# GpSimd's queue in a feature-interaction kernel: the three sums of a block first, then the gathers and stores of another block

## The reference

```python
e = jnp.stack([tbl_0[ids[:, 0]], ..., tbl_39[ids[:, 39]]], axis=1)      # 512 x 40 x 32
h = e
for i, (W, bias) in enumerate(params):                                   # three layers of 200
    x = jnp.einsum('bhd,bmd->bhmd', h, e).reshape(B, -1, D)
    y = jax.nn.relu(jnp.einsum('oi,bid->bod', W, x) + bias[None, :, None])
    if i != n_layers - 1:
        h, direct = jnp.split(y, 2, axis=1)
    else:
        direct = y
    outs.append(direct)
z = jnp.concatenate(outs, axis=1).sum(-1)
h = jnp.maximum(jnp.concatenate([z, dense_ctx], axis=1) @ W_top1 + b_top1, 0.0)
y = jnp.maximum(h @ W_top2 + b_top2, 0.0) @ W_top3
```

## Time and profile before

| | us |
|---|---|
| median of three runs | 2821.92 (2819.53 to 2822.87) |
| the profiled execution, its own time | 2822.93 |
| its span in the trace | 2821.1 |
| PE busy | 2775.4 (98% of the span) |
| DVE busy | 2637.9 (94%) |
| ACT busy | 1500.6 (53%) |
| GpSimd busy | 858.7 (30%) |
| DMA issued by GpSimd (queue q0), share of 16 engines | 12.1% |

### The profile page before, as it was taken

One profiled execution on the slowest core, in us unless ns is written; L12 is line 12 of the kernel. 1 busy time (PEld: TensorE's weight loads), 2 busy tenths in 40 slices (PEclk: granted clock), 3 DMA queues, 4 the chain that ended last, 5 costly groups with the idle time before them and its releaser, 6 DMA issues.

```text
span 2821.1 us, 54038 instructions
## 1 busy us (share of the span) xinstructions
PE 2775.4 (98%) x19012; PEld 2758.2 (98%) x19012; DVE 2637.9 (94%) x1945; ACT 1500.6 (53%) x1880; POOL 858.7 (30%) x700
## 2 busy tenths in 40 slices
PE   5999999999999999999999999999999999999999
PEld 4999999999999999999999999999999999999997
DVE  6999999999999999999999999999999999999995
ACT  4555555555555555555555555555555555555553
POOL 5433332332332332332323323323323323333100
PEclk9999999999999999999999999999999999999999
DMA  7333333433433433333334334334333334334330
GB/s 210 85 83 84 86 94 78 94 87 76 99 88 75 100 84 82 97 84 85 93 79 94 87 78 97 89 75 102 85 78 99 85 82 95 85 86 94 85 78 18
DMA packets 286025, 249.66 MB, mean 89 GB/s; under 512 B 31286, under 2 KB 284446, under 8 KB 285893
## 3 DMA queue, kind: packets, MB, share of 16 engines
q1 hardware_dynamic: 216310, 200.56, 25.4%
q0 software_dynamic: 65712, 45.56, 12.1%
q10 hardware_dynamic: 3972, 3.17, 0.4%
HBM read 140.74 MB, written 4.20 MB: 51 GB/s over the span
## 4 chain that ended last, share of the span: by engine, by line
PE 94%; POOL 2%; DVE 1%; DMA 1%; issue 1%; SPq 0%; ACT 0%; another core or an unknown queue 0%; DVEq 0%; ACTq 0%; POOLq 0%
PE acc L809 62%; PE acc L811 29%; POOL gathered L445 1%; PE z_ps L826 1%; PE hid_ps L822 1%; DVE tails L721 1%; DMA acc_copy<-acc_copy 1%; DVE product L716 1%; PE acc L880 0%; SPq L380 0%; DMA gathered<-in_table,rows_all 0%; PE hid_ps L903 0%; DMA hid_rep<-hid 0%; ACT acc_copy L528 0%
## 5 line engine op out<-in xcount | busy, mean ns | idle before, releaser
L809 PE MATMUL acc<-weights,heads 126*128 126x400 f32 (+1 forms) x9088 | 2694.1, 364 | 16.3 <-DVE tails L721 16.2
L811 PE MATMUL acc<-weights,tails 126*128 126x200 f32 (+1 forms) x9088 | 2321.6, 255 | 0.0
L522 ACT ACTIVATE heads<-product 126x1024 fp32r<-126x1024 f32 (+2 forms) x1152 | 1198.1, 1047 | 1021.5 <-PE acc L811 507.3
L811 PEld LDWEIGHTS acc<-weights,tails 126*128 126x128 f32 (+1 forms) x9088 | 1740.8, 192 | 0.0
L809 PEld LDWEIGHTS acc<-weights,heads 126*128 126x128 f32 (+1 forms) x9088 | 1712.9, 188 | 19.7 <-issue 10.0
L721 DVE TENSOR_TENSOR tails<-product,heads 126x1024 fp32r<-126x1024 f32 (+2 forms) x1152 | 1348.9, 1204 | 1.4 <-ACT heads L522 1.1
L716 DVE TENSOR_TENSOR product<-hid_rep,x_rep 126x2048 f32<-126x2048 f32 x510 | 1167.4, 2289 | 96.5 <-PE acc L811 64.8
L453 POOL DMA_DIRECT2D acc_copy<-acc_copy x189 | 235.0, 1244 | 1719.8 <-ACT acc_copy L528 1716.4
L445 POOL DMA_INDIRECT gathered<-in_table,rows_all x320 | 510.8, 1596 | 101.4 <-issue 97.1
L536 ACT ACTIVATE y_relu<-acc_copy 128x400 f32<-128x400 f32 x192 | 102.4, 533 | 217.0 <-DMA acc_copy<-acc_copy 215.0
L528 ACT ACTIVATE acc_copy<-acc 128x800 f32<-128x800 f32 x192 | 158.7, 827 | 9.8 <-PE acc L811 7.7
(11 more groups left out here) (26 smaller groups left out, 118.2 us busy)
## 6 DMA issues: line engine op xcount, KB each, us to landing
x_rep<-x_rows SPq DMA_DIRECT2D x512, 120.0 KB
hid_rep<-hid SPq DMA_DIRECT2D x511, 120.0 KB
x_pairs<-x_rows SPq DMA_DIRECT2D x191, 280.0 KB
acc_copy<-acc_copy POOLq DMA_DIRECT2D x189, 200.0 KB
hid_rep<-hid SPq DMA_DIRECT2D x511, 5.0 KB
x_pairs<-x_rows SPq DMA_DIRECT2D x63, 120.0 KB
gathered<-in_table,rows_all POOLq DMA_INDIRECT x320
raw_weights<-in_w SPq DMA_DIRECT2D x8, 500.0 KB, 6.1
```

Of the source, the lines that this page charges most:

```text
L522: act.activation(heads[0:rows, ring % HEADS_RING, 0:tiles, :], product[0:rows, ring % PRODUCT_RING, 0:tiles, :], ACT.Copy).then_inc(heads_ ...
L809: nc.tensor.matmul(acc[:, at.parity, c, 0:2 * LAYER], dims(heads[0:rows, ring % HEADS_RING, k, :], c), w, start=(q == 0 and k == 0), stop= ...
L811: last = nc.tensor.matmul(acc[:, at.parity, c, LAYER:2 * LAYER], dims(tails[0:rows, ring % PRODUCT_RING, k, :], c), w[:, 0:LAYER], start=F ...
```

## The change

GpSimd issues all three sums of a block before its gathers and stores. Before, the first sum stood ahead of the gathers, and the second and third between the gathers and the stores; for block 5 alone one gather stood ahead of the first sum. No instruction is added or removed, and the other engines' lists stay as they are.

```diff
             for b in range(FIRST, blocks):
                 first = 1 + (b - FIRST) * 3
-                ahead = 1 if b == FIRST + 1 else 0
-                for k in range(ahead):
-                    gather(0, k, rows_all[:, b, k:k + 1], x_gathered)
-                add(first)
-                for k in range(ahead, FLD_DMA):
+                sums_ahead = 3
+                for n in range(sums_ahead):
+                    add(first + n)
+                for k in range(FLD_DMA):
                     gather(0, k, rows_all[:, b, k:k + 1], x_gathered)
                 pool.wait_ge(x_gathered, (b - (FIRST - 1)) * GATHERS)
-                add(first + 1)
-                add(first + 2)
+                for n in range(sums_ahead, 3):
+                    add(first + n)
                 for part in stored_parts(b, 0):
                     pool.dma_start(*part).then_inc(x_stored, 16)
                 pool.wait_ge(x_stored, (b - (FIRST - 1)) * STORES)
```

## The result

The changed kernel takes 3354.83 us (median of five runs, 3350.14 to 3367.55), the kernel before 2821.57 us beside it (five runs, 2819.53 to 2822.87). The ratio is 1.1898, with a 95% interval of 1.1885 to 1.1911. The profiled execution of the changed kernel took 3367.55 us, its span is 3365.8 us, so 544.7 us longer than the 2821.1 us before, or 9.08 for each of the 60 blocks.

The account below looks back on a forecast made before the run. PE was taken as the bound, its matmuls of heads filling 2694.1 us. A stall of 7.2 us plus 1.6 us of clock made 8.8 us a step, 528 us over 60 blocks: 3350 us, range 2825 to 3520.

Parts of the forecast that it names:

- The bound and the room: PE's matmuls of heads fill 2694.1 us; moved GpSimd work must fit 16.77 us between the sums of layers 0 and 1.
- The first gather: GpSimd's first gather in the new place starts at 1249.22, waits for DVE's pause and ends at 1258.2.
- each is the first behind something other than a gather: Three gathers of 4.96 to 11.12 us at the trace's start follow other work; such gathers wait for a true DVE pause.
- The Trainium skill's rule: DVE and GpSimd share an SBUF port under exclusive lock; a gather would wait for one DVE instruction; 2840 us.
- rival (1): Each gather slips in behind one DVE instruction; layer 1's sum 1.9 us late, 18 us lost, 2840 us; chance 0.17.
- The other gathers: The four gathers behind the first take 2.35 us each, 9.4 us, to 1267.6, since DVE works on.
- Landing and stores: Behind the gathers, 1.8 us for their landing and 3.9 us for stores and their wait, ahead of layer 1's sum.
- From the sum to PE: Layer 1's sum 8.8 us late stops DVE's fold; made tails absorb 1.6 us, so PE loses 7.2 us a step.
- The clock: PE's clock drops to mostly 1.2 GHz behind each stall of 7 us, losing 1.6 us a step.
- The sum: Whole-program total: 60 gatherings at 8.8 us a step lose 528 us, giving 3350 us.

Follow-up runs that it names:

- the memset: Changed kernel plus one 128x128 DVE memset a step, behind the last product of layer 1, while the first gather waits: 2969.56 us, ratio 1.0500.
- with PE filled: Changed kernel plus 24 idle matmuls of 128x128 ahead of PE's turn of layer 1: 3282.35 us, ratio 1.1622.
- the kernel with the pause: Changed kernel, with DVE waiting about 0.6 us for heads ahead of the product of pair 4 of layer 1: 2844.04 us, ratio 1.0086.
- the run with memsets between gathers: Kernel before, with a one-element GpSimd memset behind each gather: 2824.05 us, ratio 1.0009.

## Why the prediction was right, point by point

- **The bound and the room.** Right. PE was the bound, and everything moved had to fit into 16.77 us. In the changed kernel the piece from the sum of layer 0 to the sum of layer 1 takes 1568.35 - 1538.98 = 29.4 us.
- **The first gather.** Right in size: forecast 1258.2 - 1249.22 = 9.0 us, to the start of DVE's pause plus 0.95; measured 10.6, by the same rule (all 60 ended at a pause). The reason was wrong, and this is the step that failed. The premise "each is the first behind something other than a gather" is refuted; what the runs show in its place is that it hangs on how long DVE has been at work without a pause when the gather starts. It gave the right answer because the gather's new place has a run of 8.8 us, and the old one 3.5. That is luck: with a run of up to 7.8 us no gather was held.
- **The Trainium skill's rule.** "SBUF — State Buffer", section "Who interferes with whom", has the later instruction wait until the first finishes. That fits the gathers that got in. It doesn't fit the 60 of the changed kernel, which were passed over at seven ends of DVE's instructions; its time, 2840 us, was rival (1), and the measurement decides against it. That the port is what they wait for agrees with the memset, which has no input in on-chip memory and let the gather in.
- **The other gathers.** Forecast 4 x 2.35 = 9.4 us; measured 1560.72 - 1551.09 = 9.6.
- **Landing and stores.** Forecast 1.8 + 3.9 = 5.7 us; in the block shown 1568.35 - 1560.72 = 7.6. The landing was the term that was too small: GpSimd waited 3.25 us for it, 2.22 in the block before.
- **From the sum to PE.** The size was right, the way was not. I had PE stop at the tails behind DVE's fold; it stopped at its own turn of layer 1, which waits for the relu itself. Forecast 7.2 us a block; measured 411.0 / 60 = 6.85. The sum was later than forecast: ACT's copy ended at 1557.06 and the sum went at 1568.35, 11.3 us behind it (9.3 in the block before, 0.3 in the kernel before), where I had it 8.8 late. Its landing was quicker: 1572.56 - 1568.35 = 4.2 us to the relu instead of 5.56, which gives most of that back.
- **The clock.** Forecast 1.6 us a block. PE's busy time rose from 2775.4 to 2918.9 us, 2.4 a block, with windows at 0.50 and 0.85 in which it did 16 and 25 matmuls instead of 30. Kept busy, PE gave back 1.2 a block. The term is of the right kind, and lies between these.
- **The sum.** Forecast 8.8 a block, 528 us; measured 3354.83 - 2821.57 = 533 us, 8.9 a block. Three terms that were too small (the first gather, the gathers' landing, the clock) and one too large (the sum's own landing) leave it near. That it is nearer than its parts is luck.

What stays open: whether the limit is a time (near 8.8 us) or a number of DVE instructions (behind five a gather got in; behind six most did not, and the four with PE filled did), what else decides at the limit, and why it works so. Four gathers at the starts of the traces, the one at 89.28 and one in each of three other kernels, are a case that the account doesn't cover: they were passed over at four or eight ends and then let in without a pause. A gather that follows a gather got in at the next end also over 10 us behind DVE's last pause (10.4 in the kernel with the pause), as if a gather that got in ended the run too; no run here tries that by itself.

## What to carry to other kernels

Before moving a GpSimd DMA that reads its row numbers from on-chip memory, look at what VectorE does not only beside the new place but ahead of it: two-input instructions in an unbroken row for some 9 us or more held it here, nearly always until the next pause, and a pause of 0.6 us or a memset 4 to 5 us ahead of it let it through. Don't put a piece of work whose length hangs on another engine's pauses, with two waits for landings, ahead of a short instruction that PE waits for; moving that instruction ahead of the waits gave back 458 of 533 us here, and a pause of VectorE gave back 511. When a theory explains a bimodal row, look at what differs a few microseconds earlier, not only at the moment itself.

## What the runs showed of the hardware that was not expected

- An indirect DMA on GpSimd was passed over at the ends of 6 or 7 DVE instructions (9.8 to 11.2 us), and in one case at 16 (21.8 us, at 88.53 in the run with memsets between gathers), although gathers in other places got in at the first such end. Runs of DVE of 8.76 us and more since its last pause went with the first, of up to 7.8 us with the second; four gathers at 8.8 us, with PE filled, got in as well.
- A DVE memset of 0.17 us lets a waiting gather in, and also ends the run ahead of one that has not started yet (3.7 us and at most 3.2 us instead of 10.6).
- GpSimd's direct DMAs were not held in these stretches: a sum took 1.18 to 1.21 us with DVE at work, right ahead of gathers that took 10 us.
